# Graph convolutions of a GNN kernel: a pair's two pre-activations before its two sums, squares ahead of the copies, and node ranks found by matrix products

## The reference, cut to what matters

```python
m = jnp.concatenate([x[dst], x[src], ea], axis=-1) @ w1 + b1      # per edge, 128 wide
m = jax.nn.silu(group_norm(m, g, bt))                             # 8 groups of 16
m = m @ w2 + b2
out = jax.ops.segment_sum(m, dst, num_segments=n)
cnt = jax.ops.segment_sum(jnp.ones(...), dst, num_segments=n)
return out / jnp.clip(cnt, 1.0)[:, None]
```

## Time and profile before

| | |
|---|---|
| median of 3 runs | 11735.4 us (11731.89 to 11742.31) |
| the profiled execution | 11847.9 us, of which the span of the profile 11846.2 us |
| busy, share of the span | PE 69%, PE weight loads 55%, VectorE 58%, ScalarE 35%, GpSimd 55% |
| the largest groups of GpSimd | conv gathers L537: 3232, mean 947 ns |
| `prepare` | 0 to 60 us |
| `first` | 60 to 238 us |
| convolution 1 | 238 us to about 2720 us |
| convolution 2 | starts between 2900 and 2960 us, ends about 5345 us |

### The profile page before, as it was taken

The page is one execution under the profiler, slowest core; times in us unless marked ns, Lnnn a source line. Parts: engine busy times, 40 slices in busy tenths (PEclk is TensorE's granted clock), DMA queues, the critical chain, the costliest instruction groups (busy, mean ns, idle before and its releaser), DMA issues. The chain is left out here.

```text
span 11846.2 us, 181243 instructions
## 1 busy us (share of the span) xinstructions
PE 8134.7 (69%) x44314; PEld 6471.6 (55%) x44314; DVE 6838.3 (58%) x16254; ACT 4174.9 (35%) x19386; POOL 6469.9 (55%) x6618
## 2 busy tenths in 40 slices
PE   2677777775777777774666666666467777777775
PEld 1455455553555555553555555555367667777774
DVE  4677777775777777775545555555633333333336
ACT  0344444442444444441222222222123333333332
POOL 4666666662666666642555555554155555555551
PEclk7888888887888888886777777777578788888886
DMA  4344344442434444433554444554344444444443
GB/s 109 107 113 114 112 112 114 113 114 60 113 112 114 113 113 113 113 97 107 144 146 144 143 143 143 144 144 115 84 94 96 96 95 98 97 96 98 99 97 89
DMA packets 1667963, 1323.24 MB, mean 112 GB/s; under 512 B 578730, under 2 KB 1444339, under 8 KB 1666782
## 3 DMA queue, kind: packets, MB, share of 16 engines
q1 hardware_dynamic: 1427212, 770.46, 23.7%
q0 software_dynamic: 237088, 539.87, 17.6%
q10 hardware_dynamic: 2610, 1.32, 0.1%
HBM read 1250.67 MB, written 60.09 MB: 111 GB/s over the span
## 5 line engine op out<-in xcount | busy, mean ns | idle before, releaser
L537 POOL DMA_INDIRECT conv_gath<-b,plan x3232 | 3060.8, 947 | 2007.9 <-issue 866.6
L890 POOL DMA_INDIRECT gat_gath<-g,idx x1616 | 1756.4, 1087 | 1540.6 <-DVE gat_val L1171 861.2
L890 POOL DMA_INDIRECT attn_gath<-kv,plan x1616 | 1528.5, 946 | 1429.6 <-DVE attn_val L1171 746.3
L573 PE MATMUL conv_sums<-conv_hot,conv_m 128*128 128x128 f32 x6464 | 1271.8, 359 | 1261.0 <-ACT acc L610 553.5
L573 PEld LDWEIGHTS conv_sums<-conv_hot,conv_m 128*128 128x128 f32 x6464 | 1100.2, 257 | 1670.5 <-issue 1670.4
L593 ACT ACTIVATE conv_sq<-conv_z 128x512 f32<-128x512 f32 x808 | 482.2, 597 | 2276.7 <-PE conv_z L563 1917.9
L925 PE MATMUL gat_p_edge<-weta,plan 128*128 128x136 f32 x3232 | 862.8, 355 | 522.0 <-ACT gat_edge L1000 255.8
L656 DVE TENSOR_REDUCE conv_var<-conv_sq 128x32 f32<-128x512 f32 x808 | 549.4, 680 | 1153.2 <-ACT conv_sq L593 960.5
L560 PEld LDWEIGHTS conv_z<-conv_win,conv_hotT 128*128 128x128 f32 x6464 | 923.1, 205 | 514.0 <-issue 514.0
L1025 ACT COPY small<-attn_smalls 40x127 f32 x1616 | 417.3, 258 | 1987.8 <-remote 1490.4
L556 PE MATMUL conv_z<-conv_wblock,conv_ea 128*128 128x512 f32 x1616 | 988.1, 698 | 82.6 <-DVE conv_hotT L647 37.9
(11 more groups left out here) (370 smaller groups left out, 15956.4 us busy)
## 6 DMA issues: line engine op xcount, KB each, us to landing
conv_win<-a SPq DMA_DIRECT2D x3232, 64.0 KB
conv_places<-places SPq DMA_DIRECT2D x202, 512.0 KB
attn_win<-q SPq DMA_DIRECT2D x1616, 64.0 KB
plan<-in_xeT SPq DMA_DIRECT2D x404, 256.0 KB
conv_gath<-b,plan POOLq DMA_INDIRECT x3232
attn_places<-places SPq DMA_DIRECT2D x101, 512.0 KB
plan<-places SPq DMA_DIRECT2D x404, 128.0 KB
attn_gath<-kv,plan POOLq DMA_INDIRECT x1616
```

The source lines that it names most:

```text
L537: pool.indirect_dma_start(gath[:, b.c * BQ + k, t, :], None, b_table, bass.IndirectOffsetOnAxis(ap=C["src"][:, b.quad(k) * QT + t:b.quad(k ...
L573: mm = nc.tensor.matmul(sums[g % SQ][:, t * P:(t + 1) * P], m[:, g % BQ, t * P:(t + 1) * P], hot[:, g % BQ, t, :], start=True, stop=True)
L890: pool.indirect_dma_start(gath[:, b.c * BQ + k, t, :], None, table, bass.IndirectOffsetOnAxis(ap=rows, axis=0))\
```

## The change

Three edits, in one diff.

1. TensorE issues both pre-activations of a pair, then both sums.
2. ScalarE issues in step p: the register loads when due, square(2p+4), square(2p+5), copies(2p-2), silu(2p), copies(2p-1), silu(2p+1). Its last step falls away. The copies belong to a pair one later than before.
3. The ranks: `prepare` loads the tile starts with one batch on each partition, twice, shifted by one batch (`starts_k`), and makes from them the steps between the batches. A comparison of 101 x 6272 elements says which batch a node has reached (`reached`); 49 small products of TensorE with `steps` give each node the starts of its own batch and its number. VectorE reads them from PSUM and finds the tile, in the same two parts, still in `prepare`. The 49 gathers of L1785 and `find_tiles` in `first` are gone; the 49 gathers of L1791 start at once, and the first `rank` moves from behind group 5 to behind group 4.

```diff
@@ prepare: SP
             sp.wait_ge(padded, 1)
+            by_batch = w["n0_b"].rearrange("o (k t) -> (o k) t", t=TB)
+            sp.dma_start(starts_k[:, 0, :], by_batch).then_inc(starts_loaded, 16)
+            sp.dma_start(starts_k[1:NBATCH, 1, :], by_batch[0:NBATCH - 1, :]).then_inc(starts_loaded, 16)
+            sp.wait_ge(padded, 2)
             for dst, src in edge_loads:
@@ prepare: POOL
+            pool.iota(nodes_i[:, :], pattern=[[1, NP]], base=0, channel_multiplier=0).then_inc(nodes_made, 1)
@@ prepare: TensorE
+            pe.wait_ge(reached_made, 1)
+            for part, (b0, b1) in enumerate(RANKED):
+                for b in range(b0, b1):
+                    mm = nc.tensor.matmul(p_n[part][:, (b - b0) * (TB + 1):(b - b0 + 1) * (TB + 1)],
+                                          reached[:, b * P:(b + 1) * P], steps[:, :], start=True, stop=True)
+                mm.then_inc(starts_ready, 1)
             pe.wait_ge(loaded, LOADS)
@@ prepare: VectorE
+            nc.vector.memset(starts_k[0:1, 1, :], 0).then_inc(padded, 1)
             nc.vector.memset(dst_q[:, :], N).then_inc(padded, 1)
...
+            dve.wait_ge(starts_loaded, 2 * 16)
+            link(nc.vector.tensor_copy(first_k[:, :], starts_k[:, 0, 0:1]))
+            link(nc.vector.memset(first_k[0:1, :], -1.0))
+            link(nc.vector.tensor_tensor(steps[:, 0:TB], starts_k[:, 0, :], starts_k[:, 1, :], ALU.subtract))
+            link(nc.vector.memset(steps[:, TB:TB + 1], 1.0))
+            dve.wait_ge(nodes_made, 1)
+            link(nc.vector.tensor_scalar(reached[:, :], nodes_i[:, :], first_k[:, 0:1], None, ALU.is_gt))
+            dve.sem_inc(reached_made, 1)
             dve.wait_ge(edges_loaded, EDGE_LOADS)
-            link(nc.vector.tensor_copy(n0_f[:, :], n0_all[:, :].rearrange("p (k t) -> p k t", t=TB)[:, :, 0]))
-            link(nc.vector.tensor_tensor(below[:, :, 0:NBATCH], bc(n0_f[:, :].unsqueeze(1), wide),
-                                         bc(node[:, :].unsqueeze(2), wide), ALU.is_lt))
-            link(nc.vector.tensor_reduce(batch[:, :], below[:, :, 0:NBATCH], AX.X, ALU.add))
-            link(nc.vector.tensor_scalar(batch[:, :], batch[:, :], -1.0, 0.0, ALU.add, ALU.max))
-            link(nc.vector.tensor_copy(batch_i[:, :], batch[:, :]))
...
             dve.sem_inc(places_made, 1)
+            for part, (b0, b1) in enumerate(RANKED):
+                bs, wide = slice(b0, b1), [P, b1 - b0, TB]
+                dve.wait_ge(starts_ready, part + 1)
+                pn = p_n[part][:, 0:(b1 - b0) * (TB + 1)].rearrange("p (b t) -> p b t", t=TB + 1)
+                link(nc.vector.tensor_tensor(below[:, bs, 0:TB], pn[:, :, 0:TB], bc(node[:, bs].unsqueeze(2), wide), ALU.is_lt))
+                link(nc.vector.tensor_reduce(tile[:, 0, bs], below[:, bs, 0:TB], AX.X, ALU.add))
+                link(nc.vector.scalar_tensor_tensor(tile[:, 0, bs], pn[:, :, TB], float(TB), tile[:, 0, bs], ALU.mult, ALU.add))
+                link(nc.vector.tensor_scalar(tile[:, 0, bs], tile[:, 0, bs], -1.0 - TB, 0.0, ALU.add, ALU.max))
+                link(nc.vector.tensor_copy(tile_i[:, bs], tile[:, 0, bs]))
@@ conv_edges: TensorE
             for p in range(-2, NPAIR + 1):
                 pre_activation(2 * p + 4)
+                pre_activation(2 * p + 5)
                 sum_up(2 * p - 2)
                 sum_up(2 * p - 1)
-                pre_activation(2 * p + 5)
@@ conv_edges: ScalarE
-            for p in range(-2, NPAIR + 2):
-                g = 2 * p - 4
+            for p in range(-2, NPAIR + 1):
+                g = 2 * p - 2
                 if g % BQ == 0 and 0 <= g < NQ:
                     starts = starts_of(nc, C, ACT_ENGINE, Batch(g // BQ // RB, g // BQ % RB))
+                square(2 * p + 4)
+                square(2 * p + 5)
                 copies(g, starts)
+                silu(2 * p)
                 copies(g + 1, starts)
-                silu(2 * p)
-                square(2 * p + 4)
                 silu(2 * p + 1)
-                square(2 * p + 5)
@@ node_stage, kind "first": POOL
                 for part, (b0, b1) in enumerate(RANKED):
-                    for b in range(b0, b1):
-                        pool.indirect_dma_start(n0_rows[:, b, :], None, w["n0_b"].rearrange("o (k t) -> (o k) t", t=TB),
-                                                bass.IndirectOffsetOnAxis(ap=batch_i[:, b:b + 1], axis=0))\
-                            .then_inc(n0_gathered[part], 16)
-                for part, (b0, b1) in enumerate(RANKED):
-                    pool.wait_ge(tile_found, part + 1)
                     for b in range(b0, b1):
                         pool.indirect_dma_start(dst_rows[:, b, :], None, w["dst_r"].rearrange("o (t e) -> (o t) e", e=P),
@@ node_stage, kind "first": VectorE
                     step(g, g % 2, g - 1 if g else None, None)
-                    if g == 1:
-                        find_tiles(dve, link, 0)
-                    if g == 3:
-                        find_tiles(dve, link, 1)
-                    if g == 5:
+                    if g == 4:
                         rank(dve, link, 0)
```

More of the change, by code:

```diff
@@ L203, in prepare @@
         node_i = st.sb("node_i", [P, NBLK], I32)
-        n0_f = st.sb("n0_f", [P, NBATCH])
-        node, below, batch, batch_i = (R[n] for n in ("node", "below", "batch", "batch_i"))
+        starts_k = st.sb("starts_k", [NBATCH, 2, TB], I32)
+        first_k = st.sb("first_k", [NBATCH, 1])
+        steps = st.sb("steps", [NBATCH, TB + 1])
+        nodes_i = st.sb("nodes_i", [NBATCH, NP], I32)
+        reached = st.sb("reached", [NBATCH, NP])
+        node, below, tile_i = (R[n] for n in ("node", "below", "tile_i"))
         tile, shift, corner = (R[n] for n in ("tile", "shift", "corner"))
@@ L226, in prepare @@
         p_rep = st.ps("p_rep", [P, 512])
+        p_n = [st.ps(f"p_n{n}", [P, 512]) for n in range(2)]
+        starts_loaded, nodes_made, reached_made, starts_ready = (
+            st.sem(n) for n in ("starts_loaded", "nodes_made", "reached_made", "starts_ready"))
         edges_loaded, loaded, stored = st.sem("edges_loaded"), st.sem("loaded"), st.sem("stored")
@@ L366, in _ @@
             link = Chain(dve, chain)
-            wide = [P, NBLK, NBATCH]
+            nc.vector.memset(starts_k[0:1, 1, :], 0).then_inc(padded, 1)
             nc.vector.memset(dst_q[:, :], N).then_inc(padded, 1)
@@ L1377, in node_stage @@
         if kind == "first":
-            n0_gathered, dst_gathered = ([st.sem(f"{n}{h}") for h in range(2)] for n in ("n0_gathered", "dst_gathered"))
-            tile_found, ranked, degree_ready, rank_chain = (
-                st.sem(n) for n in ("tile_found", "ranked", "degree_ready", "rank_chain"))
+            dst_gathered = [st.sem(f"dst_gathered{h}") for h in range(2)]
+            ranked, degree_ready, rank_chain = (st.sem(n) for n in ("ranked", "degree_ready", "rank_chain"))
         LOADS = 16 * {"first": 1, "conv1": 0, "conv2": 1, "attn": 3, "gat": 3}[kind]
@@ L1748, in node_stage @@
         if kind == "first":
-            node, below, batch, tile = (R[n] for n in ("node", "below", "batch", "tile"))
-            n0_rows, dst_rows, batch_i, tile_i, degree = (R[n] for n in ("n0_rows", "dst_rows", "batch_i", "tile_i", "degree"))
-            def find_tiles(dve, link, part):
-                b0, b1 = RANKED[part]
-                bs = slice(b0, b1)
-                dve.wait_ge(n0_gathered[part], (b1 - b0) * 16)
-                wide = [P, b1 - b0, TB]
-                link(nc.vector.tensor_tensor(below[:, bs, 0:TB], n0_rows[:, bs, :], bc(node[:, bs].unsqueeze(2), wide), ALU.is_lt))
-                link(nc.vector.tensor_reduce(tile[:, 0, bs], below[:, bs, 0:TB], AX.X, ALU.add))
-                link(nc.vector.scalar_tensor_tensor(tile[:, 0, bs], batch[:, bs], float(TB), tile[:, 0, bs], ALU.mult, ALU.add))
-                link(nc.vector.tensor_scalar(tile[:, 0, bs], tile[:, 0, bs], -1.0, 0.0, ALU.add, ALU.max))
-                link(nc.vector.tensor_copy(tile_i[:, bs], tile[:, 0, bs]))
-                dve.sem_inc(tile_found, 1)
+            node, below, tile = (R[n] for n in ("node", "below", "tile"))
+            dst_rows, tile_i, degree = (R[n] for n in ("dst_rows", "tile_i", "degree"))
             def rank(dve, link, part):
@@ L1858, in build @@
             R = {"node": kept("node", [P, NBLK]), "below": kept("below", [P, NBLK, P]),
-                 "n0_rows": kept("n0_rows", [P, NBLK, TB], I32), "dst_rows": kept("dst_rows", [P, NBLK, P], I32),
-                 "batch": kept("batch", [P, NBLK]), "batch_i": kept("batch_i", [P, NBLK], I32),
+                 "dst_rows": kept("dst_rows", [P, NBLK, P], I32),
                  "tile": kept("tile", [P, 2, NBLK + 1]), "tile_i": kept("tile_i", [P, NBLK], I32),
```

## The result

The kernel after takes 11648.6 us in the median of four runs (11643.7 to 11670.2), the kernel before 11738.0 (four runs, 11731.9 to 11742.3): a ratio of 0.9928, 95% interval 0.9911 to 0.9945, that is -89 us. The forecast was 11673 us, -62. The profiled execution of after has a span of 11648.4 us and a mean clock of 0.818; that of before had 11846.2 and 0.794. These spans differ by 198 us, the medians by 89: before's profiled execution lay 110 us, 0.93%, above its median, after's does not, and this has to be borne in mind wherever two stages are set side by side.

What follows compares the result with a forecast made beforehand. Runs of POOL gathers, with TensorE's signals unseen until about 2.0 us afterwards, bound the convolutions. Terms -7.7 (`prepare`), -54.6 (`first`) and 0 (order) gave -62, taken off the median: 11673 us, range 11,420 to 11,770.

Steps and rivals of the forecast that it cites:

- The lock: In the convolutions, TensorE's signals are seen only about 2.0 us after POOL's last gather, giving eight gathers per 11.94 us period.
- The order of the convolutions, 0 us: TensorE's and ScalarE's new order in the convolutions: the run of eight gathers still decides, with 3 us slack; 0 us.
- A: Faster rival: in the convolutions the gathers don't lock, or it loosens; -751 us, smaller form -248; chance 0.18.
- B: Slower rival: in the convolutions, runs break into four gathers and 2.0 us is paid twice; +751 us, chance 0.12.
- the hold: In the convolutions, TensorE's signals stay unseen during a run of gathers, until about 2.0 us after its last gather.
- The chain laid out from a release: In the convolutions, the next pre-activations end 6.7 and 11.4 us after a release, in time for the 11.94 us period.
- `prepare`, -7.7: Stage `prepare`: 11.4 us of batch search leaves VectorE's path, 3.7 us of tile search is added; net -7.7 us.
- a sign of being wrong: The forecast named VectorE waiting at the second tile search in `prepare` as showing it wrong; it expected no wait.
- `first`, -54.6: Stage `first`: 49 gathers of 1.25 us go, so the convolution starts at 184.0 us, not 238.64: -54.6 us.
- C: Same-time rival: the ranks don't pay in `first` and slower convolution starts take the rest; 11,710 to 11,760 us, chance 0.08.
- The rule weighed: In the convolutions, idle gaps return TensorE to half clock, up to 0.9 us per instruction pair; slack absorbs it, 0 us.
- the slow rival: In the convolutions, POOL's runs break into four gathers, paying 2.0 us twice; +751 us, chance 0.12.

## Why the prediction was right, and what of it was not

*The lock.* It stands as read: the squares follow POOL's last gather by 1.85 to 1.94 us in the rows of after, 191 of the 195 runs of each convolution have eight gathers, and without gathers the pair falls to VectorE's 9.9. The forecast called it "read off the order of time, not explained". That stays so: the runs show that gathers are needed for it and that not every chip has it, not what does the holding.

*The order of the convolutions, 0 us.* No kernel of the study shows a large effect, and A (full, -751; smaller, -248) and B (+751) are out. The size is -7 without the hold and +17 with it, alone; the third chip's difference (-30 with the ranks, which are worth -53 to -60) says +23 to +30. Of this some 7 us a convolution are in the period of the runs, and some 2 in the rest, with one or two more runs of four at the start. That the sum's 0 came so close is in part luck, for the working had two faults that nearly cancel: it left out that the signals leave one by one, so that the new order puts the pre-activations first and POOL starts 0.13 us sooner (time from the first signal to the gather 0.39 to 0.40 us in the old order, 0.27 to 0.34 in the new); and that the hold itself is longer in the new order on the third and fourth chips, 1.95 and 1.93 us on average in convolution 1 from the last gather to the first signal, against 1.85 and 1.87 in the old order on the third and fifth. On the first chip it isn't (1.86 for 1.90), so the second fault can be the chip's or the execution's. The chain laid out from a release was out of phase too: in the kernel after the pair's two pre-activations end 3.3 and 8.7 us (middle values) after POOL starts again, where it had 6.7 and 11.4. Both are in time for the next run, so the run of eight decides, as forecast.

*The first chip's -89.* With the ranks as measured and the order as forecast, the change should have given -53 + 0. The two traces give -53 for the start, -50 for the two convolutions, -7 for the stages behind them, -87 for unchanged code. Before's profiled execution was 0.93% above its median; with 0.93% taken off its stages (2418.6 becomes 2396.1), the convolutions of the two kernels are within 4 us, and some -28 us remain in attention and GAT, which the change doesn't touch. That correction assumes that the execution was slow evenly, which isn't shown, nor is it known that it ran on the chip of the median. So what the -36 beyond the ranks are on that chip stays open: two profiles can't settle it, and the order alone wasn't run there. That it is a general gain of the order is excluded by the fourth chip.

*`prepare`, -7.7.* Measured -4.6 (first gather 61.22 to 56.66). L388 came 11.6 us earlier, the tile searches took 3.6, iota and comparison were hidden: as worked out. TensorE's 49 products are the mis-sized term: taken at 16 us, half of the bound 33, they took 21.1, so that VectorE waited 3.45 us at the second tile search, which the forecast had named as a sign of being wrong. Half of a bound was a guess. The 98 instructions of 17 columns follow each other at 0.21 us with a weight load of 0.33 us each. In convolution 1 the 128-wide L588 has just these numbers where the granted clock is 0.50 (1530.71), and 0.11 and 0.19 us where it is full (1534.56). So the few columns saved nothing, and the products ran at the pace of the half clock; the profile has no record of the clock that early.

*`first`, -54.6.* From its first gather to convolution 1 the stage took 177.4 us and takes 128.7, -48.7. 49 gathers went, 61 us; the last copy came 50.4 us after group 1's (forecast 50.0) and the convolution 9.5 behind it (9.6). What was mis-sized is the release after a long run of gathers: 2.0 us assumed, 7.0 us measured. The short runs' 2.0 doesn't carry over. Without the hold, on the second chip, POOL's first gather of convolution 1 came 58 us earlier, though no copy waits for gathers there.

*C.* The ranks pay on every chip where their effect can be read (-53 to -60), so C is out as a mechanism, though the third chip's -30 for the whole change is its size: by the order's +17 on the fourth chip, it is the order that takes back part of what the ranks give. The forecast's -62 was 3 + 6 us too much in the ranks, and the measured -89 lies beyond it by what the ranks don't explain.

*The rule weighed.* The half clock lasts longer than the one or two rows that the forecast gave it: in the rows of after the granted clock is 0.50 from 1529 to 1533 us, and nearly the whole first pre-activation runs at it, L584 in 1.92 us and L588 in 1.91, 4.9 us in all; the second has 1.02 and 1.05, and 2.8 in all. It still ends before the release, so it costs nothing, and the granted clock of the stage went from 0.86 to 0.90. What the rule would have made of it, the slow rival, didn't come.

## What to carry to other kernels

When a wait names an engine, compare the end of its instruction with the start of the one that waited, in two neighbouring periods: a distance that jumps (0.11 and 3.30 us) while another engine's stays (2.03 and 2.04) says whose end really counts. A change of a few tenths of a per cent should be split into its parts and each timed on more than one chip: here one part is worth -57 and -60 wherever it was timed, and the other -7 on one chip and +17 on another. Don't take stages of two single profiles as the gain before their own times stand beside the medians.

## What the runs showed of the hardware

- The same kernel takes 11738, 9298, 11812, 11808 and 11811 us on five chips. On the second, TensorE's semaphore updates come 0.014 us behind the product while POOL gathers; on the others many come only when a run of gathers is over, the first on average 1.85 to 1.95 us behind its last gather, and the others mostly 0.09 to 0.15 us apart. Why one chip doesn't do it isn't known.
- Behind a run of 49 gathers the first copy of a product came 7.0 us later (7.4 and 7.5 on the third and fifth chip), not 2.0. It isn't the landing of the data that ends the hold: in the kernel after the last packet of the gathers' queue is through at 119.59 us, and the signal of a product that ended at 103.94 rises at 125.34.
- A signal is sometimes let go within a run: in the kernel after, that of a sum that ended at 1529.22 rose at 1535.47, one microsecond before the run's last gather began.
- An indirect gather of 128 rows on POOL repeats every 1.25 us on all five, whatever else differs.
